# Mixer in half-tile steps, with GpSimd normalising the probabilities before they are turned

## The chip, the cores and the metric

One core of a Trainium2 chip runs the kernel. The metric is the device time of one execution in microseconds (us), the median of several executions; here 940.95 us. The engines are named as in the profile: PE (TensorE's matmuls), PEld (its weight loads), DVE (VectorE), ACT (ScalarE), POOL (GpSimd) and SP (SyncE, which only issues transfers). All five run their own instruction lists in order and meet at semaphores.

## The reference, cut to what matters

A small language model on 16 sequences of 128 tokens, width 192: embedding with layer norm, an attention block, then a block that begins with the *mixer*, a self-attention of 12 heads of 16 within each sequence, and ends in a dense layer pair and four gated experts. The change touches the mixer alone:

```python
h = _ln(x, ln1_g, ln1_b)
qkv = h @ in_w.T + in_b                       # E = 192, H = 12 heads, D = 16
q, k, v = jnp.split(qkv, 3, axis=-1)
scores = jnp.einsum('bqhd,bkhd->bhqk', q, k) / jnp.sqrt(jnp.float32(D))
attn = jax.nn.softmax(scores, axis=-1)
ctx = jnp.einsum('bhqk,bkhd->bqhd', attn, v).reshape(B, N, E)
x = x + ctx @ out_w.T + out_b
```

## The kernel before, in words

Three functions follow each other in one program, each a block of its own at whose end all engines meet: `attention`, `mixer` (L776), `experts`. The mixer works on 16 tiles of 128 tokens (a tile is a whole sequence, so a token attends within its tile), in 4 units of 4 tiles. The work is cut into named steps; one list, `order`, holds them, and `walk_order` lets each engine run its share of every step in the order of that list. So the list alone sets the order of every engine's instructions; GpSimd has a list of its own in the kernel before.

Steps for a unit: **N** (parts 0 to 2: DVE scales the rows of the next unit, multiplies by a gain, adds a shift and copies a piece; part 3: DVE normalises the residual rows and adds a bias), **X** (PE transposes the 4 tiles in two parts, ACT copies each to a rounded half, DVE subtracts to get the other half), **Q0**, **Q1**, **Q2** (PE projects queries and keys; ACT takes Q0 and a part of Q2, DVE takes Q1 and the rest of Q2), **V0** to **V3** (PE projects the values of one tile, DVE adds the bias).

Steps for a tile t: **S** (PE: 8 score matmuls into 4 strips of 3 heads, `scores`; DVE: one maximum for each strip, L1145; ACT: 12 exponentials with their sums, L1047), **T** (PE turns the 12 blocks of probabilities, L979; ACT copies them out, L1058), **I** (DVE takes the reciprocal of the 12 sums, L1150; PE spreads it over rows by 12 small matmuls, 24 instructions in the profile at L989; ACT copies the result, L1053), **A** (PE: `mix`, probabilities times values, L1002; DVE multiplies by the spread reciprocals while it copies, L1158), **O** (PE: output projection, L1011; DVE adds to the residual `hin`, L1162). Beside them **L** (DVE: statistics and two inverse roots of the last unit's rows, in 11 parts) and **W** (DVE: the low halves of the dense weights of the later stage, L1111, 15 parts in all).

Tile t's list is T(t-1), I(t-1), S(t), A(t-1), the projections and N of the next unit, W, L, O(t-1). The scores of tile t wait for all exponentials of tile t-1, since there is one buffer of scores (4 PSUM banks) and one of probabilities. The PSUM results of X, Q, V, T, I, A and O go through a ring of 4 banks in the order of the list; a step waits until the bank's last user has been copied out.

GpSimd loads the five sets of dense weights, each by four transfers that it issues itself (L912 to L914), waits until they have landed, and writes the rounded halves (L916 to L918); before the next set it waits for DVE's three W parts. In the attention stage GpSimd also normalises that stage's probabilities (L450).

Of the kernel before, what the change touches and what calls it, by code (L numbers as in the profile page):

```python
# [775 lines left out]
def mixer(nc, keep, dram):  # L776
# [9 lines left out]
    PAIR = 2 * HD  # L786
    with ExitStack() as ctx:
# [18 lines left out]
        probs = sb("probs", [P, STRIPS, SETS, P])  # L806
        pt = sb("pt", [P, STRIPS, SETS, P])
        sums, inverse = (sb(n, [P, STRIPS, SETS]) for n in ("sums", "inverse"))
        inverse_rows = sb("inverse_rows", [P, SETS, P])
# [8 lines left out]

        order = []
# [4 lines left out]
        def inputs(unit, parts):  # L824
            order.extend(("N", (unit, part)) for part in parts)

        LAST_NORM = 1 + TWICE_PARTS
        projections(0, "X Q0 Q1 Q2")
        for t in range(TILES + 1):
            unit, j = divmod(t, UNIT)  # L830
            if t:
                order.extend((("T", t - 1), ("I", t - 1)))
            if t < TILES:
                order.append(("S", t))
            if t:
                order.append(("A", t - 1))
            if t == 0:
                projections(0, "V0 V1 V2 V3")
            if unit + 1 < UNITS:
                inputs(unit + 1, {0: (0, 1, 2), 3: (3,)}.get(j, ()))  # L840
                projections(unit + 1, {0: "", 1: "X Q0", 2: "Q1 Q2 V0", 3: "V1 V2 V3"}[j])
            if t == 0:
                inputs(0, (3,))
            if 0 < t < TILES:
                order.append(("W", t - 1))
            if t in (1, 2):
                half_way = LAST_NORM // 2
                order.extend(("L", part) for part in (range(half_way) if t == 1 else range(half_way, LAST_NORM)))
            if t:
                order.append(("O", t - 1))  # L850
# [4 lines left out]
        for step, i in order:  # L855
            for part in range({"X": 2, "Q": 1, "V": 1, "T": STRIPS, "I": 1, "A": 1, "O": 1}.get(step, 0)):
                slot_of[step, i, part] = slots
                slots += 1
# [6 lines left out]
        turned, spread, mixed, out_filled = sem("turned"), sem("spread"), sem("mixed"), sem("out_filled")  # L865
        inverse_ready, rows_ready, q_tail_ready = sem("inverse_ready"), sem("rows_ready"), sem("q_tail_ready")
# [10 lines left out]
        for (step, i, part), slot in slot_of.items():  # L877
# [5 lines left out]
            elif step == "V":  # L883
                emptied[slot] = ((v_ready, UNIT * i[0] + i[1] + 1),)
            elif step == "T":
                emptied[slot] = ((pt_ready, STRIPS * i + part + 1),)
            elif step == "I":
                emptied[slot] = ((rows_ready, i + 1),)
# [13 lines left out]
        def _(pool):  # L902
# [4 lines left out]
            for f in range(FFNS):  # L907
                w1_hi, _, _, w2 = keep["ffn"][f]
# [6 lines left out]
                pool.wait_ge(stage_loaded, 64 * (f + 1))  # L915
                nc.gpsimd.tensor_scalar(w1_hi[:, :], stage[:, 0, :], 1.0, 1.0, ALU.mult, ALU.mult).then_inc(weights_hi, 1)  # L916
                nc.gpsimd.tensor_scalar(w1_half[:, :], stage[:, 1, :], keep["low_rows"][:, 0:1], 1.0, ALU.mult, ALU.mult).then_inc(weights_hi, 1)
                nc.gpsimd.tensor_scalar(w2[:, :, 0, :], stage2[:, :, :], 1.0, 1.0, ALU.mult, ALU.mult).then_inc(weights_hi, 1)  # L918

        @block.tensor  # L920
        def _(pe):
# [34 lines left out]
            def scores(t):  # L956
                unit, b = divmod(t, UNIT)
                if b == 0:
# [4 lines left out]
                if t:  # L963
                    pe.wait_ge(exps_ready, 2 * t)
# [3 lines left out]
                for i in range(STRIPS):  # L968
# [4 lines left out]
            def turn_probs(t):  # L973
                for i in range(STRIPS):
                    if i % 2 == 0:
                        pe.wait_ge(exps_ready, 2 * t + i // 2 + 1)
                    slot_free("T", t, i)
                    for s in range(SETS):
                        last = nc.tensor.transpose(ring[:, bank("T", t, i), s * P:(s + 1) * P], probs[:, i, s, :], keep["ident"][:, :])  # L979
                    last.then_inc(turned, 1)  # L980

            def spread_inverse(t):

                pe.wait_ge(inverse_ready, t + 1)
                slot_free("I", t)
                for s in range(SETS):
                    for i in range(STRIPS):
                        wide = inverse[:, i, s:s + 1].to_broadcast([P, PAIR])
                        last = nc.tensor.matmul(ring[32 * i:32 * i + 32, bank("I", t), s * P:(s + 1) * P], wide, keep["ident"][:, :], start=True, stop=True)  # L989
                last.then_inc(spread, 1)  # L990

            def mix(t):
# [6 lines left out]
                for s in range(SETS):  # L999
                    for i in range(STRIPS):  # L1000
                        rows = slice(32 * i, 32 * i + 32)
                        last = nc.tensor.matmul(ring[rows, bank("A", t), s * P:(s + 1) * P], v_pad[:, unit % 2, b, i * SETS + s, :], pt[:, i, s, :], start=True, stop=True)  # L1002
# [669 lines left out]
```

## Time and profile before

| | us |
|---|---|
| median of 3 runs (lowest, highest) | 940.95 (940.44, 943.34) |
| the profiled execution | 939.32 |
| its span in the profile | 937.6 |
| mixer, first to last instruction | 433.5 to 616.5 |
| busy in the span: PE, DVE, ACT, POOL | 816.1, 526.9, 487.3, 192.2 |
| mean granted clock of TensorE | 0.96 of full speed |

How to read it: the times inside the program are those of one profiled execution, counted from the start of its span. An engine's busy time is the union of its instructions' spans; idle time before an instruction is put down to the instruction that released it. Granted clock 1.00 is 2.4 GHz, 0.50 is 1.2 GHz.

### The profile page before, as it was taken

To read this page: it belongs to the slowest core of one execution; us is meant where nothing else is said; L and a number is where in the kernel's file an instruction comes from. 1 tells how busy PE (TensorE), PEld (TensorE's weight loads), DVE (VectorE), ACT (ScalarE), POOL (GpSimd) and SP (SyncE) were. 2 spreads that over 40 slices of the span, in tenths; PEclk is the share of its full clock that TensorE was granted. 3 is DMA by queue.
4 is the path that set the end of the run, shared out by engine and by line. 5 is a ranking of instruction groups with operands and counts; after the bars stand their busy time and mean duration, and the time that the engine had idled before them with its cause. 6 is when DMAs were issued, how large, how long until landed. Compare 5 with 4: busy or idle time off the path is not lost. (4 is left out here: it accounts for less than half of the span.)

```text
span 937.6 us, 16696 instructions
## 1 busy us (share of the span) xinstructions
PE 816.1 (87%) x6264; PEld 725.3 (77%) x6264; DVE 526.9 (56%) x1388; ACT 487.3 (52%) x1298; POOL 192.2 (20%) x285
## 2 busy tenths in 40 slices
PE   0599999999999999985685868669989999999997
PEld 0488999999999998974564646558878888898887
DVE  5763645454545454345666656525877556566564
ACT  2255454545353535331566757845645665576653
POOL 4561010202020202021002211200115106042070
PEclk9899999999999999997689989999999999999999
DMA  8433333333333333333001101230000000000000
GB/s 236 115 80 69 77 69 77 69 76 69 77 68 77 69 77 68 77 69 88 1 2 59 61 19 43 60 90 1 1 1 1 1 18 1 1 18 1 17 1 19
DMA packets 33617, 47.34 MB, mean 50 GB/s; under 512 B 4672, under 2 KB 28608, under 8 KB 33536
## 3 DMA queue, kind: packets, MB, share of 16 engines
q1 hardware_dynamic: 28240, 34.63, 16.1%
q0 software_dynamic: 2544, 9.05, 3.4%
q10 hardware_dynamic: 2752, 2.59, 1.1%
q8 instruction: 50, 0.82, 0.4%
q14 instruction: 31, 0.25, 0.1%
HBM read 30.53 MB, written 15.73 MB: 49 GB/s over the span
## 5 line engine op out<-in xcount | busy, mean ns | idle before, releaser
L1488 DVE TENSOR_TENSOR ffn_hid_lo<-ffn_gelu,ffn_hid_hi 128x512 fp32r<-128x512 f32 x120 | 98.0, 818 | 107.2 <-ACT ffn_hid_hi L1462 106.2
L1416 PE MATMUL ffn_ps_out<-ffn_weights_w,ffn_hid_hi 128*128 128x384 f32 x480 | 144.8, 358 | 3.5 <-DVE ffn_hid_lo L1488 3.3
L1458 ACT ACTIVATE ffn_gelu<-ffn_ring,ffn_b 128x512 f32<-128x512 f32 x120 | 82.3, 686 | 113.3 <-PE ffn_ring L1405 111.0
L1417 PE MATMUL ffn_ps_out<-ffn_weights_w,ffn_hid_lo 128*128 128x192 f32 x480 | 121.1, 252 | 0.0
L450 POOL TENSOR_SCALAR attn_probs<-attn_probs,attn_inverse 128x128 f32<-128x128 f32 x128 | 48.2, 376 | 297.2 <-DVE attn_inverse L738 289.5
L1416 PEld LDWEIGHTS ffn_ps_out<-ffn_weights_w,ffn_hid_hi 128*128 128x128 f32 x480 | 90.5, 189 | 9.8 <-DVE ffn_hid_lo L1488 4.9
L1417 PEld LDWEIGHTS ffn_ps_out<-ffn_weights_w,ffn_hid_lo 128*128 128x128 f32 x480 | 91.8, 191 | 4.2
L607 ACT ACTIVATE attn_probs<-ps_scores,attn_neg_max 128x128 f32<-128x128 f32 x128 | 45.3, 366 | 77.6 <-DVE attn_neg_max L734 77.6
L1462 ACT ACTIVATE ffn_hid_hi<-ffn_gelu 128x512 fp32r<-128x512 f32 x120 | 75.9, 633 | 3.8
L1047 ACT ACTIVATE mix_probs<-mix_ps_scores,mix_neg_max 128x128 f32<-128x128 f32 x192 | 67.4, 392 | 17.5 <-DVE mix_neg_max L1145 17.5
L1346 POOL TENSOR_SCALAR ffn_bias_part<-ffn_b,ffn_gates 128x192 f32<-128x192 f32 x64 | 37.4, 600 | 135.8 <-DVE ffn_gates L1522 134.7
L1405 PE MATMUL ffn_ring<-ffn_xt_hi,ffn_weights_w_hi 128*128 128x512 f32 x120 | 52.2, 435 | 5.2 <-DVE ffn_xt_lo L1484 5.2
L745 DVE COPY attn_mixed_rows<-ps_pairs 128x256 f32<-128x256 f32 x32 | 13.6, 425 | 75.4 <-PE ps_pairs L538 49.0
L1145 DVE TENSOR_REDUCE mix_neg_max<-mix_ps_scores 128x3 f32<-128x384 f32 x64 | 31.2, 551 | 39.1 <-PE mix_ps_scores L970 39.1
L553 PE MATMUL ps_scores<-w_proj_main,attn_mixed_rows 128*128 128x192 f32 x256 | 49.2, 326 | 2.2 <-issue 2.1
L621 ACT ACTIVATE attn_mixed_rows<-ps_mixed 128x512 f32<-128x512 f32 x32 | 19.2, 599 | 60.3 <-PE ps_scores L553 33.6
L598 ACT ACTIVATE attn_q_main<-ring,attn_b_qk 128x256 f32<-128x256 f32 x64 | 30.4, 475 | 37.2 <-PE ring L485 33.6
L1405 PE MATMUL ffn_ring<-ffn_xt_lo,ffn_weights_w_hi 128*128 128x512 f32 x120 | 48.4, 403 | 0.0
L1405 PE MATMUL ffn_ring<-ffn_xt_hi,ffn_weights_w_lo 128*128 128x512 f32 x120 | 48.0, 400 | 0.0
L1405 PE MATMUL ffn_ring<-ffn_xt_hi,ffn_weights_w_stack 128*128 128x512 f32 x120 | 47.7, 398 | 0.0
L1405 PE MATMUL ffn_ring<-ffn_xt_lo,ffn_weights_w_stack 128*128 128x512 f32 x120 | 47.4, 395 | 0.0
L979 PE MATMUL mix_ring<-ident,mix_probs 128*128 128x128 f32 x192 | 29.3, 291 | 20.4 <-DVE hin L1162 9.6
(272 smaller groups left out, 2152.6 us busy)
## 6 DMA issues: line engine op xcount, KB each, us to landing
v_rows<-attn_v_flat SPq DMA_DIRECT2D x16, 768.0 KB, 3.3
attn_v_rows<-v_rows SPq DMA_DIRECT2D x128, 96.0 KB, 3.7
mix_stage<-in_w POOLq DMA_DIRECT2D x5, 576.0 KB, 5.7
mix_stage<-in_w POOLq DMA_DIRECT2D x10, 192.0 KB, 3.4
mix_stage<-in_w POOLq DMA_DIRECT2D x5, 384.0 KB, 4.4
attn_stage_main<-in_w_qkv SPq DMA_DIRECT2D x2, 768.0 KB, 9.0
h_rows<-hin SPq DMA_DIRECT2D x8, 192.0 KB, 2.8
ffn_base<-h_rows SPq DMA_DIRECT2D x1, 1536.0 KB, 9.6
```

Source lines behind the costliest of these rows:

```text
L450: last = nc.gpsimd.tensor_scalar(probs[:, n, j, :], probs[:, n, j, :], inverse[:, n, j:j + 1], float(D) ** -0.5, ALU.mult, ALU.mult)
L553: last = nc.tensor.matmul(out_of(b), mixed_rows[:, c, :], w, start=c == 0, stop=c == KTILES - 1)
L607: last = nc.scalar.activation(probs[:, n, j, :], ps_scores[:, n % 2, j, :], ACT.Exp, bias=neg_max[:, n, j:j + 1], accum_out=sums[:, n, j:j ...
L1047: last = nc.scalar.activation(probs[:, i, s, :], ps_scores[:, i, s * P:(s + 1) * P], ACT.Exp, bias=neg_max[:, i, s:s + 1], accum_out=sums[ ...
L1145: nc.vector.tensor_reduce(out=neg_max[:, i, :], in_=ps_scores[:, i, 0:WIDE].rearrange("p (s k) -> p s k", k=P), op=ALU.max, axis=X, negate ...
L1346: last = nc.gpsimd.tensor_scalar(bias_part[:, b, :], b2[:, 1 + e, :], gates[:, b, e:e + 1], 1.0, ALU.mult, ALU.mult)
L1405: last = nc.tensor.matmul(ring[:, bank("L1", i), :], w[:, cols], x[k][:, part, :], start=n == 0, stop=n == 4)
L1416: nc.tensor.matmul(ps_out[:, b, 0:2 * D], hid_hi[:, i % 3, tile], w2[:, c, :, :], start=c == 0, stop=False)
L1417: last = nc.tensor.matmul(ps_out[:, b, 0:D], hid_lo[:, i % 3, tile], w2[:, c, 0, :], start=False, stop=c == HC - 1)
L1458: nc.scalar.activation(gelu[:, i % 2, :], ring[:, bank("L1", i), :], ACT.Gelu, bias=b1[:, f * HC + c:f * HC + c + 1]).then_inc(chunk_read, 1)
L1462: nc.scalar.activation(hid_hi[:, i % 3, :], gelu[:, i % 2, :], ACT.Copy).then_inc(hi_ready, 1)
L1488: nc.vector.tensor_tensor(hid_lo[:, i % 3, :], gelu[:, i % 2, :], raw(hid_hi[:, i % 3, :]), ALU.subtract).then_inc(lo_ready, 1)
```

## The change

The mixer's list is written in *steps of half a tile*: step h handles two of the four strips (6 of the 12 head blocks) of tile h//2; there are 32, and 4 more to drain. S, T and the new E (ACT's exponentials), P (ACT's copies of the turned probabilities), J (DVE's reciprocal of 6 sums) and Z (new: GpSimd multiplies the 6 blocks of probabilities by their reciprocals) run by halves; A and O stay by tiles. The spreading step I is gone with its 24 PE instructions and its ACT copy, and A's copy on DVE is a plain copy. Probabilities, turned probabilities and sums have two buffers. GpSimd now walks the same list: its weight loads become G (the issues) and H (the three rounded halves), put between its Z steps.

```diff
+        order.append(("S", 0))
+        projections(0, "V0 V1 V2 V3")
+        order.append(("G", 0))
+        for h in range(HALVES + 4):
+            unit, j = divmod(h, UNIT_HALVES)
+            more = unit + 1 < UNITS
+            first = h % 2 == 0
+            if 1 <= h <= HALVES:
+                order.extend((("J", h - 1), ("Z", h - 1)))
+            if h + 1 < HALVES:
+                order.append(("S", h + 1))
+            if 2 <= h < HALVES + 2:
+                order.append(("T", h - 2))
+            if first and 4 <= h:
+                order.append(("A", (h - 4) // 2))
+            if not first and 5 <= h:
+                order.append(("O", (h - 5) // 2))
+            if h < HALVES:
+                order.append(("E", h))
+            if 2 <= h < HALVES + 2:
+                order.append(("P", h - 2))
+            if 0 < unit < UNITS:
+                projections(unit, {0: "V1", 1: "V2", 2: "V3"}.get(j, ""))
+            if more:
+                projections(unit + 1, {2: "X", 3: "Q0", 4: "Q1", 5: "Q2", 7: "V0"}.get(j, ""))
+            if not first and 5 <= h:
+                order.append(("D", (h - 5) // 2))
+            if more:
+                order.extend(("N", (unit + 1, part)) for part in {0: (0, 1), 1: (2,), 6: (3,)}.get(j, ()))
+            if h == 0:
+                order.append(("N", (0, 3)))
+            f, part = divmod(h - 2, SPLIT_STEPS)
+            if part == 0 and 0 < f < FFNS:
+                order.append(("G", f))
+            if part in (2, 3, 4) and 0 <= f < FFNS:
+                order.append(("H", 3 * f + part - 2))
+            if part in (3, 4, 5) and 0 <= f < FFNS:
+                order.append(("W", 3 * f + part - 3))
+            if 2 <= h < 6:
+                order.extend(("L", part) for part in range((h - 2) * LAST_NORM // 4, (h - 1) * LAST_NORM // 4))
...
+            def normalise(h):
+                pool.wait_ge(inverse_ready, h + 1)
+                for i in range(h % 2 * HALF, (h % 2 + 1) * HALF):
+                    for s in range(SETS):
+                        turn = probs[:, h // 2 % 2, i, s, :]
+                        last = nc.gpsimd.tensor_scalar(turn, turn, inverse[:, i, s:s + 1], 1.0, ALU.mult, ALU.mult)
+                last.then_inc(probs_ready, 1)
...
+                if h >= 2:
+                    pe.wait_ge(exps_ready, h - 1)
...
+            def turn_probs(h):
+                pe.wait_ge(probs_ready, h + 1)
+                for part, i in enumerate(strips_of(h)):
+                    slot_free("T", h, part)
                     for s in range(SETS):
...
-            def spread_inverse(t):
-
-                pe.wait_ge(inverse_ready, t + 1)
-                slot_free("I", t)
-                for s in range(SETS):
-                    for i in range(STRIPS):
-                        wide = inverse[:, i, s:s + 1].to_broadcast([P, PAIR])
...
+            def invert(h):
+                mine = slice(h % 2 * HALF, (h % 2 + 1) * HALF)
+                dve.wait_ge(exps_ready, h + 1)
+                if h >= 2:
+                    dve.wait_ge(probs_ready, h - 1)
+                nc.vector.reciprocal(inverse[:, mine, :], sums[:, h // 2 % 2, mine, :]).then_inc(inverse_ready, 1)
...
+            def take_context(t):
                 dve.wait_ge(mixed, t + 1)
...
+                nc.vector.tensor_copy(context[:, :, :], ring[:, bank("A", t), 0:WIDE].rearrange("p (s k) -> p s k", k=P)).then_inc(context_ready, 1)
```

## Rows read from the trace of the kernel before

**Rows 1.** The page of the profile, part 1: each engine's busy time and its share.
```profile
PE 816.1 (87%) x6264; PEld 725.3 (77%) x6264; DVE 526.9 (56%) x1388; ACT 487.3 (52%) x1298; POOL 192.2 (20%) x285
```

**Rows 2.** Stretches of the mixer: busy us of each engine (instructions), granted clock, DMA share, GB/s.
```profile
433.50:445.30 11.80, 8.13 (x23) 6.11 (x24) 5.20 (x12) 3.32 (x5) 4.60 (x8) 0.61 0.58 158
445.30:496.70 51.40, 38.04 (x361) 31.35 (x361) 34.02 (x97) 29.19 (x120) 3.44 (x6) 0.77 0.00 1
496.70:540.50 43.80, 30.29 (x375) 24.43 (x371) 26.26 (x54) 29.16 (x121) 11.04 (x12) 0.94 0.21 64
540.50:582.70 42.20, 30.17 (x375) 24.70 (x371) 26.07 (x54) 29.17 (x121) 5.35 (x7) 0.91 0.11 34
582.70:616.50 33.80, 23.20 (x365) 18.28 (x358) 17.10 (x34) 25.89 (x117) 6.13 (x7) 1.00 0.14 42
```

**Rows 3.** Timeline (start us, us, instruction, idle before): scores of tiles 0, 14 and 15.
```profile
445.33 0.71 PE L967 MATMUL mix_ps_scores<-mix_k_main,mix_q_main 32*128 32x256 f32 x8 [1.85 <-ACT mix_k_tail L1041]
...
598.34 0.71 PE L967 MATMUL mix_ps_scores<-mix_k_main,mix_q_main 32*128 32x256 f32 x8
599.29 1.95 DVE L1145 TENSOR_REDUCE mix_neg_max<-mix_ps_scores 128x3 f32<-128x384 f32 x4 [2.14 <-PE mix_ps_scores L970]
605.84 0.71 PE L967 MATMUL mix_ps_scores<-mix_k_main,mix_q_main 32*128 32x256 f32 x8
```

**Rows 4.** Timeline, last tile: turns, mixing, its copy, output projection, its addition.
```profile
611.75 0.88 PE L979 MATMUL mix_ring<-ident,mix_probs 128*128 128x128 f32 x6 [0.59 <-ACT mix_probs L1047]
613.27 0.86 PE L1002 MATMUL mix_ring<-mix_pt,mix_v_pad 128*32 128x128 f32 x24
614.20 0.56 DVE L1158 TENSOR_TENSOR mix_context<-mix_ring,mix_inverse_rows 128x384 f32<-128x384 f32 x1 [2.25 <-PE mix_ring L1002]
614.81 1.24 PE L1011 MATMUL mix_ring<-mix_w_out,mix_context 128*128 128x192 f32 x6 [0.68 <-DVE mix_context L1158]
616.09 0.36 DVE L1162 TENSOR_TENSOR hin<-mix_ring,hin 128x192 f32<-128x192 f32 x1 [1.33 <-PE mix_ring L1011]
```

**Rows 5.** Timeline: unit 3's transposes, its split on ScalarE and VectorE, its first projection.
```profile
552.03 1.09 PE L933 MATMUL mix_ring<-ident,norm_zn 128*128 128x128 f32 x8
556.04 1.15 ACT L1026 ACTIVATE mix_zt_hi<-mix_ring 128x512 fp32r<-128x512 f32 x2
556.74 1.29 DVE L1116 TENSOR_TENSOR mix_zt_lo<-mix_ring,mix_zt_hi 128x512 fp32r<-128x512 f32 x2 [3.00 <-ACT mix_zt_hi L1026]
558.18 0.77 PE L944 MATMUL mix_ring<-mix_zt_hi,w_mix_hi 128*128 128x512 f32 x1 [5.05 <-DVE mix_zt_lo L1116]
```

**Rows 6.** Timeline, attention stage: a reciprocal and normalisations by GpSimd, four to a group.
```profile
261.27 0.17 DVE L738 RECIPROCAL attn_inverse<-attn_sums 128x4 f32<-128x4 f32 x1
...
265.61 3.53 POOL L450 TENSOR_SCALAR attn_probs<-attn_probs,attn_inverse 128x128 f32<-128x128 f32 x8 [2.25 <-DVE attn_inverse L738]
```

**Rows 7.** Timeline: GpSimd's half of a weight alone, and beside a VectorE subtraction.
```profile
445.46 0.90 POOL L917 TENSOR_SCALAR mix_w_half<-mix_stage,low_rows 128x768 fp32r<-128x768 f32 x1
...
504.25 1.70 POOL L917 TENSOR_SCALAR mix_w_half<-mix_stage,low_rows 128x768 fp32r<-128x768 f32 x1
504.30 0.96 DVE L1111 TENSOR_TENSOR ffn_weights_w_lo<-mix_stage,ffn_weights_w_hi 128x768 fp32r<-128x768 f32 x1 [0.72 <-POOL ffn_weights_w_hi L916]
```

**Rows 8.** Timeline, GpSimd: one round of weight loads and its first use (in brackets the wait).
```profile
528.67 1.10 POOL L912 DMA_DIRECT2D mix_stage<-in_w  x2 [21.61 <-DVE ffn_weights_w L1111]
...
536.14 0.82 POOL L916 TENSOR_SCALAR ffn_weights_w_hi<-mix_stage 128x768 fp32r<-128x768 f32 x1 [4.96 <-DMA mix_stage<-in_w]
```

**Rows 9.** Timeline, VectorE: two steps of the mixer's input, and the query and key tails.
```profile
451.14 1.24 DVE L181 TENSOR_SCALAR norm_zn<-hin,norm_moments,norm_both 128x192 f32<-128x192 f32 x4
452.42 0.96 DVE L184 TENSOR_TENSOR norm_zn<-norm_zn,norm_gain 128x768 f32<-128x768 f32 x1
...
478.32 1.50 DVE L1130 TENSOR_SCALAR mix_q_tail<-mix_ring,mix_b_qk 64x512 f32<-64x512 f32 x2
```

**Rows 10.** Timeline: the mixing of tile 0, at the lower granted clock.
```profile
460.20 1.51 PE L1002 MATMUL mix_ring<-mix_pt,mix_v_pad 128*32 128x128 f32 x24
```

More of the change, by code:

```diff
@@ L805, in mixer @@
         neg_max = sb("neg_max", [P, STRIPS, SETS])
[L806 to L809, printed above, removed]
+        probs = sb("probs", [P, 2, STRIPS, SETS, P])
+        pt = sb("pt", [P, 2, STRIPS, SETS, P])
+        sums = sb("sums", [P, 2, STRIPS, SETS])
+        inverse = sb("inverse", [P, STRIPS, SETS])
         context = sb("context", [P, SETS, P])
@@ L822, in projections @@
             order.extend(("X", unit) if s == "X" else (s[0], (unit, int(s[1:]))) for s in steps.split())
-        def inputs(unit, parts):
-            order.extend(("N", (unit, part)) for part in parts)
-        LAST_NORM = 1 + TWICE_PARTS
         projections(0, "X Q0 Q1 Q2")
[L829 to L850, printed above, removed]
@@ L854, in mixer @@
         slot_of, slots = {}, 0
         for step, i in order:
-            for part in range({"X": 2, "Q": 1, "V": 1, "T": STRIPS, "I": 1, "A": 1, "O": 1}.get(step, 0)):
+            for part in range({"X": 2, "Q": 1, "V": 1, "T": HALF, "A": 1, "O": 1}.get(step, 0)):
                 slot_of[step, i, part] = slots
@@ L885, in mixer @@
             elif step == "T":
-                emptied[slot] = ((pt_ready, STRIPS * i + part + 1),)
-            elif step == "I":
-                emptied[slot] = ((rows_ready, i + 1),)
+                emptied[slot] = ((pt_ready, HALF * i + part + 1),)
             elif step == "A":
@@ L905, in _, with load_weights @@
             nc.gpsimd.memset(v_pad[:, 1, :, :, HD:PAIR], 0.0).then_inc(pads_ready, 1)
-            for f in range(FFNS):
-                w1_hi, _, _, w2 = keep["ffn"][f]
+            def normalise(h):
[5 more added lines that the diff above has]
+                last.then_inc(probs_ready, 1)
+            def load_weights(f):
                 if f:
@@ L914, in _, with weight_his @@
                 pool.dma_start(stage2[:, :, :], dram["w2"][f].rearrange("(c p) n -> p c n", p=P)).then_inc(stage_loaded, 16)
[L915 to L918, printed above, removed]
+            def weight_his(i):
+                f, part = divmod(i, 3)
+                w1_hi, _, _, w2 = keep["ffn"][f]
+                if part == 0:
+                    pool.wait_ge(stage_loaded, 64 * (f + 1))
+                    nc.gpsimd.tensor_scalar(w1_hi[:, :], stage[:, 0, :], 1.0, 1.0, ALU.mult, ALU.mult).then_inc(weights_hi, 1)
+                elif part == 1:
+                    nc.gpsimd.tensor_scalar(w1_half[:, :], stage[:, 1, :], keep["low_rows"][:, 0:1], 1.0, ALU.mult, ALU.mult).then_inc(weights_hi, 1)
+                else:
+                    nc.gpsimd.tensor_scalar(w2[:, :, 0, :], stage2[:, :, :], 1.0, 1.0, ALU.mult, ALU.mult).then_inc(weights_hi, 1)
+            walk_order({"Z": normalise, "G": load_weights, "H": weight_his})
         @block.tensor
@@ L954, in project_v, with scores @@
                 last.then_inc(v_filled, 1)
-            def scores(t):
+            strips_of = lambda h: range(h % 2 * HALF, (h % 2 + 1) * HALF)
+            def scores(h):
+                t = h // 2
                 unit, b = divmod(t, UNIT)
-                if b == 0:
+                if h % UNIT_HALVES == 0:
                     pe.wait_ge(q_main_ready, unit + 1)
@@ L1001, in mix @@
                         rows = slice(32 * i, 32 * i + 32)
-                        last = nc.tensor.matmul(ring[rows, bank("A", t), s * P:(s + 1) * P], v_pad[:, unit % 2, b, i * SETS + s, :], pt[:, i, s, :], start=True, stop=True)
+                        last = nc.tensor.matmul(ring[rows, bank("A", t), s * P:(s + 1) * P], v_pad[:, unit % 2, b, i * SETS + s, :], pt[:, t % 2, i, s, :], start=True, stop=True)
                 last.then_inc(mixed, 1)
@@ L1012, in project_out @@
                 last.then_inc(out_filled, 1)
-            walk_order({"X": transposes, "Q": project_qk, "V": project_v, "S": scores, "T": turn_probs, "I": spread_inverse, "A": mix, "O": project_out})
+            walk_order({"X": transposes, "Q": project_qk, "V": project_v, "S": scores, "T": turn_probs, "A": mix, "O": project_out})
         @block.scalar
```

69 lines of the change are left out of this document (30 added, 39 removed).

## The prediction, before the changed kernel was built or run

> **What bounds the kernel now.** I read the page first: PE is busy for 87% of the span, every other engine for far less [rows 1]. That average hides the stage that is changed, so next the stretches [rows 2]: the mixer's start-up, then its four units. They last 51.4, 43.8, 42.2 and 33.8 us, and in the two middle ones no engine is busy for more than 30.3 of them. The mixer is bound by waits. The timeline shows two. First, a tile's loop: from the scores of tile 14 to those of tile 15 is 7.5 us [rows 3], because scores, maxima (first one 0.95 us after the scores), exponentials, reciprocal and spreading follow each other with nothing of the next tile between. Second, the tile in which a unit's rows are transposed: PE ends X at 553.1, ACT gets to it only at 556.0, behind the twelve exponentials that its list has first, and PE stands still for 5.05 us before the projection [rows 5]. The middle units pay 10.5 to 11 us a tile for this, the last, without projections, under 8.5.
>
> **The change part by part.** I call step h and step h+1 with odd h a *double step*: it holds one A, one O and all work of one tile. The sum is made by walking DVE's and GpSimd's lists with durations of rows.
>
> *What is removed.* 24 PE instructions and an ACT copy a tile, and with them a link in the loop. PE is then busy some 5 us less a unit than its 30 [rows 2], ACT 2 less than its 29.2 (estimates from the like mixing, 0.86 us a tile, and a copy of half a microsecond). Neither is bound, so this is worth nothing by itself.
>
> *What is split.* The loop's waits lie a step apart: S(h+1) needs only the exponentials of h-1, and E(h) the maxima made a step earlier. ACT's 27 us a unit no longer set the pace. X's copies stand behind six exponentials instead of twelve, and Q0 a step later.
>
> *What is added.* GpSimd normalises 12 blocks a tile. In the attention stage eight such blocks took 3.53 us, 0.44 each [rows 6], so Z costs 2.65 a step, 21.2 a unit. H adds 0.82, 0.90 and about 1.1, G 2.5 of issuing (528.67 to 536.14 less the 4.96 of waiting [rows 8]); with six steps for a set of weights, GpSimd has 28.5 us of work a unit where it had 3 to 11. DVE gains four reciprocals a unit, about 1 us; its copy in A reads the same 384 elements as the product did (0.56 [rows 4]); by the element rate of L184 a copy would take 0.48, by that of the tails 0.56 [rows 9], so I cost that at nothing, with a gain of 0.08 a tile as the other end.
>
> *The new wait.* Mixing A stands behind the turn T(h-2) in PE's list, T(h-2) waits for Z(h-2), and Z(h-2) for the reciprocal J(h-2), which DVE reaches only at the start of step h-1. DVE's copy of the mixing then stands ahead of everything else that DVE does in step h: values, splits, projections, norms, weights. So each double step has a chain that GpSimd is part of: J and its way to GpSimd 0.4 (261.27 to the next issue, about 0.2 beyond the reciprocal's end [rows 6]; estimate), Z 2.65, to PE 0.1 (estimate), six turns 0.8 until A starts, A to its copy 0.93, copy 0.55 [rows 4]: **5.4 us**. Behind it comes the rest of that step on DVE: after j=0 values and two N parts, 0.3 + 1.24 + 0.96, 2.6 with gaps [rows 9]; after j=2 values and X, through ACT, 2.4 (0.7 from ACT's start to DVE's, then 1.29 [rows 5]); after j=4 Q1, 2.1 (its projection about 0.6 past the copy, then as much as Q2's 1.50 [rows 9]); after j=6 N part 3, 2.2. Four double steps are 4 x 5.4 + 9.3 = 30.9 us, a unit.
>
> *On top of it, four things.* (a) W parts behind the copy: four between steps 9 and 30, 0.95 each [rows 7], 3.8. (b) GpSimd and DVE in each other's way: L917 took 0.90 alone and 1.70 beside a DVE subtraction of 0.96 whose inputs both lie in SBUF [rows 7], so such an instruction costs GpSimd about 0.8 when it meets Z. In odd steps Z is on the chain, and N part 2, W parts and their 1.35 us third parts meet it there: 0.8 in each of steps 9, 11, 23 and 29, 1.5 in 17 (two of them), 1.2 in each of 19 and 25, in all 7.1 (from below nothing, if short blocks slip between). The Trainium skill (SBUF — State Buffer, Who interferes with whom) says that a VectorE instruction with two SBUF inputs and a GpSimd one that reads SBUF shut each other out for the whole instruction; the trace agrees for 0.8 of 0.96, and by the rule's whole instruction the sum would be about 1.4 us longer. (c) G in GpSimd's queue pushes the next Z: 1.2 at G2, 0.3 at G3, 2.0 at G4 and 0.6 from the backlog after it, 4.1. The loads' landing, 4.96 us after the last issue [rows 8], is covered by the two Z between G and H. (d) One double step (13, 14), in which DVE's own instructions are longer than the chain, 0.8.
>
> *The sum.* Start: X and Q are as before, so S(0) starts at 445.3 [rows 3]. Unit 0 is DVE's: 34.0 us busy now [rows 2]; until the end of step 8 the new list adds tile 4's maxima 2.0, five more reciprocals 1.3 and the next unit's N 2.2, and I take 2.2 for gaps between dependent instructions (estimate), 41.7. Waits in it: 3.6 until V0 to V3 are through, 3.5 before the first X (Z(0), turns and transposes at the lower clock), 3.5 before Q1 likewise, 1.6 before the copy of tile 2: 12.2. So step 9 starts at 445.3 + 53.9 = 499.2. From there eight double steps of units 1 and 2, of which the last has only a value behind its copy (61.8 - 2.3), three of unit 3 (16.5): 76.0; with (a) to (d) 15.8: 91.8, step 31 at 591.0. The drain is longer than before: J(31) waits for the last W, GpSimd does two Z (7.9 us after 591.0), then turns and copies 1.6, A and its copy, O and its addition as in [rows 4], 3.2: **12.7**. The mixer ends at 603.7 instead of 616.45. Nothing behind it changes (`experts` starts where all engines meet), so the gain is 12.7 us: 939.3 - 12.7 = 926.6 against the profiled execution's own time, and 940.95 - 12.7 = **928** against the median, which lies 1.6 above it.
>
> **The rivals.**
> *A: the queue hides the chain.* If DVE's copies never wait, DVE's 29 us a unit (26.2 busy [rows 2], a microsecond of reciprocals, gaps) and GpSimd's 28.5 bound units 1 and 2, GpSimd's 3.5 a step the rest: 499 + 58 + 21 + 12 = 590, **915**. For it: every engine then has slack of a step. Against: the list puts T ahead of A, and DVE takes steps in order.
> *B: no lock.* Chain as forecast, but (b) is nothing, nor its share in unit 0 and the drain: 9 us less, **919**. For it: the attention stage's normalisations kept to 0.44 beside busy DVE [rows 6]. Against: [rows 7].
> *C: GpSimd becomes the bound, and the normalising isn't hidden.* 28.5 us, all two-input DVE work of a unit (7.2), and the scaling with one SBUF input (2.5), if that is shut out too: 38 us a unit. Units 1 and 2 then take 76 instead of 69.6, the rest about 4 more: **939**, no change. For it: GpSimd is the only engine whose work triples. Against: nothing yet shows one-input work in its way.
> *D, slower: PE's clock.* The granted clock was 0.77 in unit 0, 0.91 to 0.94 in the middle and 1.00 in the last, where PE is busy in nearly the same share (23.2 of 33.8) but with short pauses [rows 2]; it is low after pauses like the 5.05 us [rows 5]. At 1.2 GHz mixing takes 1.51 us instead of 0.86 [rows 10, 4]; on the chain that is 0.65 for A, 0.55 for T (same ratio), and about 0.55 for V, X or Q behind it, 1.75 a double step. In all eleven of them and the drain: 21 more, **950**. It decides from seven at half clock (12.7 / 1.75). For it: PE now waits once a double step for GpSimd. Against: the chain leaves it about 3 us there, less its own work. The Trainium skill (TensorE: Matmul & The Clock Gate, HAM oscillation) says that bursts with pauses between them cost the clock even where the work in them is dense; it would speak for D, the last unit's 1.00 against it.
>
> **How the numbers follow.** Forecast, 922 to 934: 0.50. A 0.15, B 0.15, C 0.11, D 0.09. The range of 8 in 10 takes in A's 915 and C's 939 with about 2 us around them, 913 to 942, and leaves out D and a little on both sides. A measurement of this kernel tells 0.3% (2.8 us) from no change. Faster, under 938.1: the forecast, A, B and a part of C, 0.82. Same: the rest of C and a little of D, 0.09; slower 0.09.
>
> **What would show it.** Right: step 9's reciprocal near 499; double steps of about 8 us in units 1 and 2, longer by 0.8 to 1.5 where N part 2 or W lies in an odd step; DVE's idle time ended mostly by the mixing, and PE's before the turns by GpSimd's normalising; normalisations of 0.44 apart, some stretched to over 1 us beside L184, L186 and L1111 work; GpSimd busy for about 85% of units 1 and 2; a mixer that ends near 604. Wrong: DVE without idle time (A), no stretched normalisation (B), GpSimd without idle time (C), a granted clock of about 0.6 in units 1 and 2 (D). The prediction also fails if unit 0, where several small waits are estimates, is off by more than 5 us.

## The result, and the profile after

The changed kernel takes 925.7 us (median of 4, 920.0 to 929.0); the kernel before took 941.4 beside it (4 runs). The ratio is 0.9835, 95% interval 0.9807 to 0.9864: 15.7 us gained, where 12.7 were forecast. The profiled execution took 925.93 with a span of 924.2. The mixer now ends at 604.0 instead of 616.5, and what follows it is 320.2 us long (321.1 before). That second part is the same in all kernels here and took 316.5 to 322.4 us in the profiled executions, so the time of a single execution moves by a few microseconds without the mixer.

The stretches of the mixer in the profile after (columns as in [rows 2]; the start-up, unit 0 to step 9, units 1 and 2, unit 3 to step 31, drain):

```profile
434.80:446.40 11.60, 7.03 (x24) 5.30 (x24) 5.10 (x12) 3.32 (x5) 3.92 (x7) 0.71 0.68 161
446.40:497.70 51.30, 38.92 (x282) 32.35 (x282) 39.45 (x108) 31.90 (x141) 24.13 (x55) 0.73 0.04 10
497.70:532.30 34.60, 29.37 (x277) 23.92 (x276) 26.03 (x58) 26.86 (x117) 24.34 (x56) 0.95 0.20 68
532.30:568.10 35.80, 29.00 (x266) 23.20 (x266) 25.75 (x54) 26.23 (x115) 27.43 (x57) 0.90 0.12 40
568.10:590.40 22.30, 19.35 (x181) 15.86 (x180) 12.61 (x30) 17.55 (x83) 17.46 (x43) 0.85 0.19 63
590.40:604.00 13.60, 9.36 (x81) 7.49 (x78) 3.91 (x9) 3.21 (x10) 6.39 (x13) 0.75 0.01 1
```

From step 9 to step 31, 92.7 us, no engine is busy throughout: PE has the most. GpSimd, 3 to 11 us a unit before [rows 2], now works 24.3 of 34.6 and 27.4 of 35.8. PE's clock is granted at 0.95, 0.90 and 0.85, where the kernel before had 0.94, 0.91 and, in its last unit, 1.00.

One double step on the timeline (steps 11 and 12; columns as in [rows 3]): the chain from one reciprocal to the next but one.

```profile
507.09 0.18 DVE L1182 RECIPROCAL mix_inverse<-mix_sums 128x6 f32<-128x6 f32 x1
507.37 2.81 POOL L931 TENSOR_SCALAR mix_probs<-mix_probs,mix_inverse 128x128 f32<-128x128 f32 x6 [3.70 <-DVE mix_inverse L1182]
508.61 0.99 DVE L1140 TENSOR_TENSOR ffn_weights_w_lo<-mix_stage,ffn_weights_w_hi 128x768 fp32r<-128x768 f32 x1
510.24 0.88 PE L1016 MATMUL mix_ring<-ident,mix_probs 128*128 128x128 f32 x6
511.05 0.86 PE L1029 MATMUL mix_ring<-mix_pt,mix_v_pad 128*32 128x128 f32 x24
511.98 0.56 DVE L1188 COPY mix_context<-mix_ring 128x384 f32<-128x384 f32 x1 [0.61 <-PE mix_ring L1029]
515.62 0.18 DVE L1182 RECIPROCAL mix_inverse<-mix_sums 128x6 f32<-128x6 f32 x1
```

Read it downward: the reciprocal at 507.09, GpSimd's group 0.28 later, lengthened to 2.81 by the VectorE subtraction that begins inside it; the turns 0.06 behind the group's end; then the mixing (0.86 as in [rows 4]); DVE's copy 0.93 after it starts; and 3.08 behind the copy until the next reciprocal at 515.62. The waits from 446 to 604 (engine, tile and line, who released it; total us, times, longest):

```profile
POOL mix_probs L931 <- DVE mix_inverse L1182: 57.4, 18, 20.8
PE mix_ring L1016 <- POOL mix_probs L931: 24.2, 14, 4.7
DVE mix_context L1188 <- PE mix_ring L1029: 20.5, 11, 4.3
DVE hin L1192 <- PE mix_ring L1038: 8.5, 6, 2.5
```

Where DVE and ACT ended PE's waits [rows 3, 5], GpSimd does now; and GpSimd, idle itself for 57.4 us (20.8 of them before its first block), waits for DVE's reciprocal: a loop, not a full engine.

### The profile page after: what moved, and what is told of

It reads as the page before. It is cut to its first block and busy times, and to the rows that moved or that the text cites. A ratio compares the mean times of both kernels' runs of the same rounds, so it can differ in the third digit from the quotient of the medians.

```text
span 924.2 us, 16183 instructions
## 1 busy us (share of the span) xinstructions
PE 821.8 (89%) x5880; PEld 730.5 (79%) x5880; DVE 530.5 (57%) x1404; ACT 479.5 (52%) x1282; POOL 265.2 (29%) x477
## 5 line engine op out<-in xcount | busy, mean ns | idle before, releaser
L1518 DVE TENSOR_TENSOR ffn_hid_lo<-ffn_gelu,ffn_hid_hi 128x512 fp32r<-128x512 f32 x120 | 95.6, 799 | 108.6 <-ACT ffn_hid_hi L1492 107.3
L931 POOL TENSOR_SCALAR mix_probs<-mix_probs,mix_inverse 128x128 f32<-128x128 f32 x192 | 75.3, 414 | 57.5 <-DVE mix_inverse L1182 57.4
L745 DVE COPY attn_mixed_rows<-ps_pairs 128x256 f32<-128x256 f32 x32 | 13.6, 424 | 75.5 <-PE ps_pairs L538 49.0
L1016 PE MATMUL mix_ring<-ident,mix_probs 128*128 128x128 f32 x192 | 33.4, 319 | 24.4 <-POOL mix_probs L931 24.2
L1016 PEld LDWEIGHTS mix_ring<-ident,mix_probs 128*128 128x128 f32 x192 | 24.4, 160 | 30.2 <-POOL mix_probs L931 27.8
```

Of the source, the lines that this page charges most:

```text
L931: last = nc.gpsimd.tensor_scalar(turn, turn, inverse[:, i, s:s + 1], 1.0, ALU.mult, ALU.mult)
L1016: last = nc.tensor.transpose(ring[:, bank("T", h, part), s * P:(s + 1) * P], probs[:, h // 2 % 2, i, s, :], keep["ident"][:, :])
L1518: nc.vector.tensor_tensor(hid_lo[:, i % 3, :], gelu[:, i % 2, :], raw(hid_hi[:, i % 3, :]), ALU.subtract).then_inc(lo_ready, 1)
```

## The experiments

The ratio compares runs on one chip and isn't exactly the quotient of the two medians. `z_nothing` leaves out the normalising, `z_factor` halves the probabilities, and `w_one_input` leaves out a subtraction.

| kernel | median us (runs) | before, same chip | ratio (95% interval) |
|---|---|---|---|
| halves_spread | 908.7 (4) | 939.9 | 0.9685 (0.963 to 0.974) |
| z_nothing | 895.8 (4) | 939.9 | 0.9532 (0.949 to 0.957) |
| mix_first | 917.7 (4) | 939.9 | 0.9761 (0.970 to 0.982) |
| lag | 912.9 (4) | 939.9 | 0.9711 (0.967 to 0.975) |
| tile_steps | 1028.7 (4) | 941.3 | 1.0941 (1.091 to 1.097) |
| z_factor | 922.6 (4) | 941.3 | 0.9812 (0.978 to 0.984) |
| w_one_input | 918.4 (5) | 941.3 | 0.9767 (0.974 to 0.979) |
| spread_late_add | 930.4 (4) | 941.3 | 0.9903 (0.987 to 0.994) |
| spread_out_first | 915.6 (6) | 940.2 | 0.9755 (0.972 to 0.979) |
| spread_mix_first | 915.1 (5) | 940.2 | 0.9722 (0.971 to 0.974) |
| lag_mix_first | 911.3 (6) | 940.2 | 0.9689 (0.966 to 0.972) |
| lag_late_dve | 910.5 (6) | 942.9 | 0.9681 (0.964 to 0.972) |

**The two halves of the change, taken apart.** `halves_spread` keeps the half steps and undoes GpSimd's normalising; `tile_steps` does the reverse.

```diff
-                order.extend((("J", h - 1), ("Z", h - 1)))
+                order.append(("J", h - 1))
...
+            if not first and 3 <= h < HALVES + 3:
+                order.append(("I", (h - 3) // 2))
...
-                pe.wait_ge(probs_ready, h + 1)
+                pe.wait_ge(exps_ready, h + 1)
```

> The steps of half a tile are kept and GpSimd's normalising is undone: the reciprocals (two halves of a tile, J) are spread over the rows by matmuls behind the turns (step I, as in the kernel before), ACT copies them out (R), and DVE multiplies by them in the copy of the mixing. Chain theory (my forecast's: from step 9 a double step is set by reciprocal, GpSimd's six blocks, turns, mixing, DVE's copy, and what DVE does behind it): the 57 us in which GpSimd waits for the reciprocal and the 24 us in which the turns wait for GpSimd go away, turns no longer wait for a step's GpSimd work, DVE or ACT becomes the bound, and the kernel takes about 913 (908 to 918), some 12 less than the changed kernel. The double steps in units 1 to 3 take 7 to 8 us. Rival, that the gain of the change comes from the normalising ahead of the turn and the spreading that it saves (24 PE instructions and an ACT copy a tile): 930 or more, between the changed kernel and the one before.

908.7, at the low end: the half steps are worth 31 us, and normalising on GpSimd gives some 15 of them back (14 by the ratios, 17 by the medians). But which engine then binds was not as expected. Step 9 to step 31 in `halves_spread`:

```profile
491.95:575.70 83.75, 80.53 (x983) 64.22 (x982) 65.05 (x141) 73.28 (x324) 18.84 (x24) 1.00 0.19 59
```

PE, busy for 80.5 of 83.75 at full clock, not DVE (65.1) or ACT (73.3). (This execution was the fastest of its four, 902.6.) No run separates the half steps from the second buffers of probabilities and sums that they came with.

```diff
+        for t in range(TILES + 1):
...
+            if t:
+                order.extend((step, h) for step in "JZTP" for h in (2 * t - 2, 2 * t - 1))
+            if t < TILES:
+                order.extend((step, h) for step in "SE" for h in (2 * t, 2 * t + 1) if (step, h) != ("S", 0))
+            if t:
+                order.append(("A", t - 1))
...
```

> GpSimd's normalising is kept and the steps of half a tile are undone: only the list is changed, to the order of the kernel before (for tile t: reciprocals, normalising, turns and their copies of tile t-1, then scores and exponentials of t, mixing of t-1, projections, norms, weights, output projection and addition of t-1). Theory, that all of the gain comes from the half steps and that normalising ahead only adds a link: the loop from the scores of a tile to those of the next (7.5 us in the kernel before) gains GpSimd's twelve blocks (4.2 us) and loses the spreading behind the turns (under 1 us), so some 3 to 4 us on each of 15 tiles, 45 to 60 us slower than the kernel before: 985 to 1000. Rival, that normalising ahead is worth something by itself (the 24 PE instructions and the ACT copy a tile that it saves): 940 or less.

1028.7, 87 us slower than the kernel before: normalising ahead pays for nothing by itself. The size was off by 29 to 44 us: I had counted GpSimd's 4.2 us alone. What else the loop holds is read from one of its shorter turns (five of them took 16.5 us on average):

```profile
547.52 0.25 DVE L1167 RECIPROCAL mix_inverse<-mix_sums 128x6 f32<-128x6 f32 x2
547.80 4.20 POOL L916 TENSOR_SCALAR mix_probs<-mix_probs,mix_inverse 128x128 f32<-128x128 f32 x12 [13.60 <-DVE mix_inverse L1167]
552.05 1.54 PE L1001 MATMUL mix_ring<-ident,mix_probs 128*128 128x128 f32 x6 [0.55 <-POOL mix_probs L916]
555.13 1.51 PE L1014 MATMUL mix_ring<-mix_pt,mix_v_pad 128*32 128x128 f32 x24
557.07 0.55 DVE L1173 COPY mix_context<-mix_ring 128x384 f32<-128x384 f32 x1
562.15 0.35 DVE L1177 TENSOR_TENSOR hin<-mix_ring,hin 128x192 f32<-128x192 f32 x1
562.42 0.25 DVE L1167 RECIPROCAL mix_inverse<-mix_sums 128x6 f32<-128x6 f32 x2
```

Reciprocals to reciprocals, 14.9 us: twelve blocks, turns and mixing at the length of the lower clock (1.51 as in [rows 10]), and then the next reciprocals behind the addition at 562.15, because DVE takes its list in order. The kernel before had 10.5 to 11 a tile in its middle units.

**What GpSimd's work costs.**

```diff
                 pool.wait_ge(inverse_ready, h + 1)
-                for i in range(h % 2 * HALF, (h % 2 + 1) * HALF):
-                    for s in range(SETS):
-                        turn = probs[:, h // 2 % 2, i, s, :]
-                        last = nc.gpsimd.tensor_scalar(turn, turn, inverse[:, i, s:s + 1], 1.0, ALU.mult, ALU.mult)
-                last.then_inc(probs_ready, 1)
+                pool.sem_inc(probs_ready, 1)
```

> GpSimd's six multiplications a step are left out, so the probabilities stay without normalising; its semaphore is still passed on from the reciprocal to the turns, and everything else is the changed kernel. Chain theory: the 2.1 us of the six blocks (2.8 to 3.6 where they are stretched) leave each of the 11 double steps and the drain, and the double steps are then as long as DVE's own instructions or the rest of the chain: about 12 to 14 us less than the changed kernel, 912. Rival, that GpSimd is hidden behind the other engines and the waits named after it only show who came last: no change, 923 to 929. Rival, that the clock of PE sets the time (shorter pauses, fewer half-clock stretches): more than 14 us less, with a granted clock near 1.00 in units 1 to 3.

30 us less, twice what the chain theory allowed: I had expected a double step of 7 to 8 us, set by DVE's list, and it takes 6.7 (73.8 / 11), with PE as the fullest engine. Step 9 to step 31 here and in the changed kernel:

```profile
492.30:566.10 73.80, 70.34 (x719) 57.47 (x716) 63.54 (x141) 67.92 (x311) 19.12 (x24) 1.00 0.21 69
```

```profile
497.70:590.40 92.70, 77.72 (x720) 62.98 (x719) 64.39 (x140) 70.64 (x315) 69.23 (x156) 0.91 0.17 56
```

With GpSimd out of the way PE is busy for 70.3 of 73.8. The same 720 instructions take 77.7 in the changed kernel, 7.4 more, at a granted clock of 0.91 instead of 1.00. What is left of its 92.7 us is PE's waits:

```profile
PE mix_ring L1016 <- POOL mix_probs L931: 12.1, 9, 2.6
PE mix_ps_scores L1005 <- ACT mix_probs L1078: 2.1, 2, 1.0
PE mix_ring L1029 <- DVE hin L1192: 0.6, 2, 0.4
```

12.1, 2.1 and 0.6: with the 77.7 that is 92.5 of 92.7. So the price of GpSimd on the chain, in this execution, is 12.1 us of waits and about 7 of PE work at a lower clock; the third rival of this run named the clock and is right for that part. Another 11.8 us lie in unit 0 (51.3 against 44.9), which I had left out, and in the drain (13.6 against 8.2), for which I had counted one group of blocks. Against `halves_spread` PE's busy time differs by 10.2 us for 264 instructions, the spreading of 11 tiles, and the stretch by 10.0 (one execution of each).

**Order or throughput.** `mix_first` puts A and O ahead of T; `lag` puts T, P, A, O and D half a step later.

```diff
-            if 2 <= h < HALVES + 2:
-                order.append(("T", h - 2))
             if first and 4 <= h:
                 order.append(("A", (h - 4) // 2))
             if not first and 5 <= h:
                 order.append(("O", (h - 5) // 2))
+            if 2 <= h < HALVES + 2:
+                order.append(("T", h - 2))
```

> In the list of steps the mixing A and the output projection O go ahead of the turns T of the same half step, since they need only turns of earlier steps. Chain theory: the order T before A is what puts GpSimd's six blocks on DVE's path (DVE's copy of the mixing waits for A, A stands behind T, T waits for GpSimd). With A first the copy no longer waits for GpSimd in the step, the chain of a double step shortens by up to 2.1 us of blocks and 0.8 of turns, and DVE's or GpSimd's lists become the bound: about 918 (912 to 922); the waits of DVE for the mixing (20.5 us in the changed kernel) fall to less than half. Rival, that the length of GpSimd's work rather than its place in PE's order is what counts: no change, 923 to 929.

```diff
-            if 2 <= h < HALVES + 2:
-                order.append(("T", h - 2))
-            if first and 4 <= h:
-                order.append(("A", (h - 4) // 2))
+            if 3 <= h < HALVES + 3:
+                order.append(("T", h - 3))
             if not first and 5 <= h:
-                order.append(("O", (h - 5) // 2))
+                order.append(("A", (h - 5) // 2))
+            if first and 6 <= h:
+                order.append(("O", (h - 6) // 2))
...
```

> Turns, their copies, mixing, output projection and the addition to the residual are all put half a step later than in the changed kernel (T of half h-3 instead of h-2), so that GpSimd has a whole step more before its blocks are needed. There are 37 half steps instead of 36. Chain theory: PE's turns never wait for GpSimd in units 1 to 3; the double steps are then set by DVE's list, 7 to 8 us, and the drain is some 2 us longer: about 916 (911 to 921). Rival, that throughput of GpSimd (or another engine) sets the pace and not the order: unchanged or 2 us longer, 925 to 930.

8 and 13 us less, with GpSimd's work unchanged: a part of its cost lies in its place. PE's waits for it ahead of the turns, step 9 to step 31, first `mix_first`, then `lag`:

```profile
PE mix_ring L1016 <- POOL mix_probs L931: 6.3, 8, 1.3
```

```profile
PE mix_ring L1016 <- POOL mix_probs L931: 4.5, 3, 1.9
```

12.1 has become 6.3 and 4.5, and the stretch 86.4 and 85.2 us; how far that can be told from chance stands under `z_factor`. Both together (and D ahead of the projections):

> The kernel with GpSimd's normalising in which turns, mixing, output projection and addition come half a step later, now also with mixing and output projection ahead of the turns, and the addition ahead of the projections' DVE work. Both of these by themselves took some of GpSimd's time off the chain (917.7 and 912.9 against 925.7). Theory, that DVE's waits for the mixing that are left (6.4 us between 497 and 590 us, 2.8 for O) come from turns that still wait for GpSimd ahead of the mixing: they fall to half, 907 to 911. Rival, that GpSimd's list with its stretched groups is the bound by now: no change, 911 to 915, with GpSimd idle for under 3 us a unit.

```profile
PE mix_ring L1016 <- POOL mix_probs L931: 1.1, 2, 0.8
```

```profile
492.67:573.05 80.38, 70.49 (x725) 58.50 (x724) 65.62 (x141) 71.60 (x320) 69.81 (x151) 1.00 0.20 65
```

The waits are nearly gone, the stretch is 80.4 us, and PE's work in it is back at 70.5 us with the clock granted at 1.00, as in `z_nothing`: the 7.4 us went with the waits. The whole, 911.3 (908 to 916), can't be told from `lag`'s. About 15 us above `z_nothing` remain: 6.6 in the stretch, 5.6 in the drain (13.8 against 8.2) and 3 in unit 0 (47.8 against 44.9). In the drain DVE was given the last two halves to normalise:

> The kernel with everything from the turns on half a step later and the mixing first (911.3), in which DVE instead of GpSimd normalises the last tile's two halves (12 blocks), where DVE has little else to do. In that kernel the last group of GpSimd begins 1.7 us after its reciprocal (577.34), because the weight halves and two groups stretched to 2.8 and 2.9 us stand ahead of it, and ends at 581.12; the turns follow at 582.2 and the mixer ends 4.7 us after that. Theory, that in the drain GpSimd's list is the chain: with six blocks of about 0.2 us on DVE behind the reciprocal the last turns start at about 578.8, 3.4 us earlier, and the kernel takes 907 to 909. Rival: DVE's 2.4 us of blocks push its copies and additions, or the mixing of the tile before is the chain: 911 to 913.

No change (910.5). The last turns began at 580.8 instead of 582.2, not at 578.8, though the probabilities were ready 3 us earlier, at 577.9; and this execution's mixer had begun 1.4 earlier as a whole (first scores at 443.4 instead of 444.8), so the turns gained nothing. The mixing of tile 14, its copy and its output projection stand ahead of them on PE, as the second half of the rival said:

```profile
578.21 0.86 PE L1035 MATMUL mix_ring<-mix_pt,mix_v_pad 128*32 128x128 f32 x24 [0.67 <-ACT mix_pt L1093]
579.75 1.24 PE L1044 MATMUL mix_ring<-mix_w_out,mix_context 128*128 128x192 f32 x6
580.83 0.82 PE L1022 MATMUL mix_ring<-ident,mix_probs 128*128 128x128 f32 x6
```

**The price of a block.**

```diff
-                        last = nc.gpsimd.tensor_scalar(turn, turn, inverse[:, i, s:s + 1], 1.0, ALU.mult, ALU.mult)
+                        last = nc.gpsimd.tensor_scalar(turn, turn, inverse[:, i, s:s + 1], 0.5, ALU.mult, ALU.mult)
```

> One number changes: GpSimd's second factor is 0.5 instead of 1.0, so the probabilities and the mixing come out at half. In the attention stage, where the second factor is not 1, eight like blocks came 0.44 us apart; in the changed kernel's mixer, where it is 1.0, six blocks took 2.1 us, 0.35 apart. If the factor makes the difference, six blocks take 2.65 as in my forecast and the kernel is about 6 us longer (0.55 in each of 11 double steps), 931 to 933. Rival, that something else makes the attention stage's blocks longer (what the other engines do beside them): blocks of 0.35 and no change, 923 to 929.

```profile
516.43 2.10 POOL L931 TENSOR_SCALAR mix_probs<-mix_probs,mix_inverse 128x128 f32<-128x128 f32 x6 [1.65 <-DVE mix_inverse L1182]
```

2.10 for six blocks, as with 1.0. The factor isn't the reason; what is, stays open.

The run tells something else as well. Its instruction lists are those of the changed kernel, so it shows how far two executions lie apart. Step 9 to step 31, and PE's waits for GpSimd in it:

```profile
499.35:586.30 86.95, 75.01 (x723) 61.65 (x721) 65.05 (x141) 70.16 (x314) 68.31 (x153) 0.95 0.16 53
```

```profile
PE mix_ring L1016 <- POOL mix_probs L931: 7.6, 7, 1.5
```

86.9 us instead of 92.7, 7.6 of waits instead of 12.1, a clock of 0.95 instead of 0.91. So what GpSimd's work costs in this stretch beside `z_nothing` is 13 us in one execution and 19 in the other. The stretch of `mix_first` and its waits can't be told from this one: its gain, 8 us against the changed kernel and 5 against `z_factor`, rests on ratios whose intervals overlap with theirs. `lag` is clear of both by its interval, and `lag_mix_first` by its waits and its stretch too.

**The lock.** In the changed kernel, the group with two VectorE instructions of two SBUF inputs inside it:

```profile
532.55 3.62 POOL L931 TENSOR_SCALAR mix_probs<-mix_probs,mix_inverse 128x128 f32<-128x128 f32 x6 [2.29 <-DVE mix_inverse L1182]
533.79 0.97 DVE L186 TENSOR_TENSOR norm_zn<-norm_zn,norm_shift 128x768 f32<-128x768 f32 x1
535.07 0.94 DVE L1140 TENSOR_TENSOR ffn_weights_w_lo<-mix_stage,ffn_weights_w_hi 128x768 fp32r<-128x768 f32 x1
```

```diff
-                nc.vector.tensor_tensor(to, of, raw(hi), ALU.subtract).then_inc(weights_lo, 1)
+                nc.vector.tensor_scalar(to, of, 1.0, 1.0, ALU.mult, ALU.mult).then_inc(weights_lo, 1)
```

> The 15 DVE subtractions that make the low halves of the dense weights (two inputs in SBUF, 0.95 to 1.35 us) are replaced by a multiplication with one input and the same output, so the low halves come out as whole weights. Lock theory: GpSimd's groups beside them lose their stretching (2.81, 3.29, 2.81, 3.62, 3.27, 2.80, 3.20 in the changed kernel in steps 11, 7, 11, 17, 19, 23 and 31; now 2.1, in step 17 2.8 because of the norm's multiplication), and the chain loses 0.7 to 1.2 in each of five or six double steps, about 5 us, besides what the one-input instruction is itself shorter (at most 0.5 each, 2 to 4 us where it stands behind the copy): 916 to 921. Rival, that any DVE work stretches GpSimd's blocks, whatever its inputs: the groups stay at 2.8 or more, and only the shorter instructions are gained, 921 to 926.

```profile
503.98 2.40 POOL L931 TENSOR_SCALAR mix_probs<-mix_probs,mix_inverse 128x128 f32<-128x128 f32 x6 [2.16 <-DVE mix_inverse L1182]
505.21 0.59 DVE L1140 TENSOR_SCALAR ffn_weights_w_lo<-mix_stage 128x768 fp32r<-128x768 f32 x1
```

Neither theory: the group at 503.98 is 2.40, not 2.1 and not 2.81. Groups beside a one-input instruction of 0.54 to 0.59 us are 0.3 to 0.4 longer, beside one of 0.75 us 0.55 longer, while a tail of 0.74 us that reads PSUM (517.11 in the changed kernel) left its group at 2.11. The Trainium skill (SBUF — State Buffer, Who interferes with whom) has this: a one-input `tensor_scalar` may run in a two-port mode, and then shuts GpSimd out as a two-input instruction does; the trace agrees with the second in kind, and for the first it shows only that 768 elements took 0.59 us against the subtraction's 0.99 in the same step. By the ratios 6 us were gained against the changed kernel and 4 against `z_factor`; the runs don't divide them between the lock and the shorter instructions.

**Can the version with spreading be bettered?** D behind the next maxima; O ahead of T and I; A too.

```diff
+            if first and 6 <= h:
+                order.append(("D", (h - 6) // 2))
             if 2 <= h < HALVES + 2:
                 order.append(("T", h - 2))
...
-            if not first and 5 <= h:
-                order.append(("D", (h - 5) // 2))
```

> The kernel with half steps and spread reciprocals (no normalising on GpSimd), with the addition to the residual (D) put from the end of each odd half step to the place behind the maxima in the next even one. In that kernel DVE's largest wait between 497 and 580 us is the one for the output projection, 9.3 us in 6 waits. Theory, that DVE's order bounds it: those waits go, and it takes 5 to 9 us less than with the addition in the odd step, 900 to 904. Rival: the bank of the ring that the projection used comes free later, the turns wait for it instead (the fourth result after it takes the same bank), and nothing is gained, 907 to 912.

22 us more. The rival holds, with the mixing in the place of the turns (waits from 499 to 590):

```profile
PE mix_ring L1037 <- DVE hin L1208: 9.2, 7, 2.2
DVE mix_context L1204 <- PE mix_ring L1037: 10.9, 9, 1.7
```

A result of the ring comes into the bank that D leaves late; PE waits for D, then DVE for PE.

> The kernel with half steps and spread reciprocals, with the output projection O ahead of the turns T and the spreading I in the odd step instead of behind them, and its addition D ahead of the projections' DVE work. DVE's largest wait there is the one for O (9.3 us in 6 waits). Theory, that DVE's order bounds that kernel and PE has room: the waits for O fall under 3 us and it takes 900 to 904 (against 908.7). Rival: the turns now stand behind O and the ring's bank is held until D, so PE or ACT waits instead and nothing is gained, 906 to 912.

> As the kernel with O first, and in the even step the mixing A also ahead of the turns T. Theory: DVE's copy of the mixing waits less (3.2 us in the kernel with spread reciprocals) and it takes 898 to 903. Rival: A needs the last copies of the turned probabilities, which ACT makes at the end of the step before, and with A first PE waits for them ahead of the turns: 906 to 912, with PE waits for ACT's copies ahead of the mixing of 5 us or more.

915.6 and 915.1, where 900 to 904 and 898 to 903 were expected: no gain. Against `halves_spread` that is 6 to 7 us more by the medians; by the ratios it is 7 and 3.5, and the second interval overlaps that of `halves_spread`. DVE's wait for O did fall, to 0.7 us (497 to 585). But PE was the fullest engine there, and it now waits more. Step 9 to step 31 in `spread_out_first` (493.86 to 582.59):

```profile
PE mix_ring L987 <- DVE hin L1208: 3.4, 3, 1.9
PE mix_ps_scores L1004 <- ACT mix_probs L1087: 3.3, 3, 1.5
```

The values (L987) are the fourth result behind O, take its bank, and wait until D has emptied it; `halves_spread` had none of the first wait and 2.1 us of the second. PE is busy for 80.9 us, 0.4 more than there, and the stretch is 88.7, 5.0 more: PE's waits make up the difference, as the rival of `spread_out_first` said. The rival of `spread_mix_first`, waits of PE for ACT's copies ahead of the mixing, didn't come.

## Why the prediction was right

**Point by point.** S(0) came at 446.4 (445.3 forecast): the start-up began 1.3 later. Unit 0 took 51.3 (53.9). Step 9's reciprocal stood at 497.66 (near 499). The eleven double steps took 92.8 (91.8), the drain 13.6 (12.7), and the mixer ended at 604.0 (603.7). The mechanism is the one forecast: the turn waits for GpSimd, the mixing for the turn, DVE's copy for the mixing, and `mix_first`, `lag` and `z_nothing` each shorten it where it was said to run.

**The terms inside the 92.8 were off, in both directions.** From the starts and ends of the chain's members, summed over the eleven:

| us | forecast | measured |
|---|---|---|
| GpSimd's groups | 36.3 | 28.0 |
| reciprocal to group, group to turns, with G and H in the queue | 9.6 | 11.5 |
| turns until A starts | 8.8 | 11.1 |
| A to its copy | 10.2 | 14.1 |
| copy | 6.1 | 6.1 |
| behind the copy, with W | 20.9 | 22.1 |

*GpSimd's block* was mis-sized: 0.44 from [rows 6], 0.35 measured, 6.0 us too much over 66 blocks. *The lock* was right in kind and nearly in price: 0.69 to 0.84 for an instruction of 0.97 to 0.99, 1.2 for one of 1.35, 1.51 for two, each less than the whole instruction; only five of the seven groups I had named met one, so 4.9 and not 7.1 us.

*The clock* made up for a part of it. Rival D was given 9%, as the whole of PE's work at 1.2 GHz; a part of it happened:

```profile
500.83 0.98 PE L1016 MATMUL mix_ring<-ident,mix_probs 128*128 128x128 f32 x6 [1.80 <-POOL mix_probs L931]
501.74 1.51 PE L1029 MATMUL mix_ring<-mix_pt,mix_v_pad 128*32 128x128 f32 x24
```

After a wait of 1.80 for GpSimd the turns take 0.98 and the mixing behind them 1.51, the length at the lower level [rows 10], 0.65 more than in [rows 4]. I had priced the chain at the upper level throughout, and the table's two PE lines, 6.2 too low, are this step's failure: three mixings and two groups of turns ran so, 3.3 us, and the rest is copies that found DVE busy and mixings that waited for a bank. So the sum came out well by errors of opposite sign, 8.3 too much for GpSimd and 9.3 too little for all else. That they cancel to within 1.0 is chance: in the execution of `z_factor` the same eleven double steps took 86.9, with 26.8 for GpSimd's groups.

**The removal of the spreading** I had called worth nothing, since PE wasn't bound. In the changed kernel PE waits, so that may stand; no run adds the spreading to it. But the reading was of the kernel before: with GpSimd off the path PE is the fullest engine, and the 24 instructions a tile cost 0.93 us each tile, 10 us in eleven double steps (`halves_spread` against `z_nothing`).

**The rivals.** A (915, the queue hides the chain) is near what `lag` makes of it, 912.9; but there PE is the fullest engine (75.8 of 85.2 us), not DVE (66.2) or GpSimd (69.4). B (no lock) and C (GpSimd the bound) fall by the stretched groups and by GpSimd's busy shares of 70% and 77% (I had forecast 85). D fell as a whole, with clocks of 0.85 to 0.95 where it needed about 0.6, and held in part.

## What to carry to other kernels

Work given to an idle engine is free only if nobody stands behind it in an in-order list: ask which wait it puts ahead of what, and move the consumer half a step later before you judge the engine's load. Where an engine is bound by waits, what it is relieved of may be worth nothing until the wait goes, and then nearly its full time (here 10.0 of 10.2 us). Price a chain at both clock levels, since each new wait on PE can also slow the work behind it. And look at a second execution of the same lists before you read a few microseconds out of one trace: here they differed by 6 in 90.

## What the hardware showed that was not expected

GpSimd's multiplications of the same shape start 0.447 us apart in the attention stage and 0.347 apart in the mixer, in one execution (both 0.37 long). The second factor isn't the cause (`z_factor`); nothing here shows what is.

```profile
L931 POOL TENSOR_SCALAR mix_probs<-mix_probs,mix_inverse 128x128 f32<-128x128 f32 x192 | 75.3, 414 | 57.5 <-DVE mix_inverse L1182 57.4
```

The mean of 414 ns in this group view of the mixer (columns: busy us, mean ns of one, idle before) hides two things: the blocks overlap, so that it overstates what an undisturbed one costs, and the longest, 1.5 us, stood beside VectorE work on SBUF alone.
